# Second attention of a four-block kernel: the first batch's output projection issued inside steps 50 to 63 of the score loop instead of steps 64 to 68

## The chip, the cores and the metric

The kernel runs on one core of a Trainium2 chip, as one program of five engines (TensorE, VectorE, ScalarE, GpSimd and SyncE, in the trace PE, DVE, ACT, POOL and SP) that wait for each other through semaphores. The metric is the device time of one execution in microseconds.

## What is computed

Four blocks are applied in turn to x of 2 x 512 x 256 floats, each as `x = x + layernorm(block(layernorm(x)))`: a linear attention, a mixture of experts, a softmax attention and a second mixture of experts. The change is in the third:

```python
qkv = jnp.einsum('bsd,df->bsf', x, Wqkv) + bqkv
...
scores = jnp.einsum('bqhd,bkhd->bhqk', q, k) / np.sqrt(HEAD_DIM).astype(np.float32)
attn = jax.nn.softmax(scores, axis=-1)
out = jnp.einsum('bhqk,bkhd->bqhd', attn, v).reshape(bsz, seqlen, D_MODEL)
return jnp.einsum('bsd,de->bse', out, Wo) + bo
```

There are 32 query heads of width 8 over 8 key heads, and 512 positions in each of the 2 batches. The last line is the output projection.

## The kernel before

The 1024 rows of x are eight tiles of 128 rows; tiles 0 to 3 (TB = 4) are the first batch, 4 to 7 the second. In the softmax attention the 64 head and batch pairs are taken four at a time (GH = 4), in NG = 16 groups n, and every group has four steps c, one for each tile of queries or keys. STEPS is 64. All engines walk the same written order of steps c = 0 to 72 (END = STEPS + LAG + 3), with d = c - 6:

- `scores1(c, i)` on TensorE makes the scores of two heads (queries by keys) in one PSUM bank each, and VectorE's `maximum` (L1744) reads each for the row maxima. This ends with step 63.
- GpSimd splits the maxima, and TensorE turns them with q (`turn`, L1594: kinds "q1", "q2", "k" and "o").
- `scores2(d, i)` makes the scores again the other way round (keys by queries, maxima included), ScalarE takes exp of each (L1505), and `weigh(d - 2, half)` (L1634) multiplies by the values into one accumulating bank.
- Every fourth step ScalarE copies a finished group's sums to `oT` (L1495), TensorE turns them (kind "o"), and VectorE divides them into `xn` (`outputs`, L1751, L1752), which from here on holds the attention's output. Group 7, the first batch's last, is in `xn` at step 40.

In a step TensorE has the order scores1 of heads 0 and 1, scores2 of two heads, half a weigh, a turn where there is one, scores1 of heads 2 and 3, an "o" turn where there is one, scores2 of the other two heads, the rest of the weigh. PSUM has eight banks. Banks 0, 1, 2 and 5 (`DVE_BANKS`) form a ring in which what VectorE reads rotates: four score tiles a step and every fourth step an "o" turn. The list `FOR_DVE` is that ring's order, and `wait_bank` makes TensorE wait until the item four places earlier has been read. Banks 3, 4 and 7 are a second ring, for ScalarE.

The output projection has four pieces for each tile t: `turn_att(t)` on TensorE (L1651, two transposes of xn's tile), a copy to `xT` (`copy_att`, L1762, by VectorE for the first batch; L1508 by ScalarE for the second), `project(t)` on TensorE (L1665, two float32 products, shown by the trace as four), and `l1_y(t)` on VectorE (L1758, which adds the bias), followed by the layernorm's statistics (L666). For the first batch `turn_att(t)` stands at the end of step 64 + t and `project(t)` at the end of step 65 + t, both behind weigh, in banks 0 to 2 that the maxima no longer use. `close_stats`, GpSimd's `rstd` (L531) and `sum_x` (L695) then update x for the first batch; its statistics (`stats_x(0)`) and ScalarE's `normalise(3, 0)` (L979) come after the loop. The second batch's projection follows the loop.

Of the kernel before, what the change touches and what calls it, by code (L numbers as in the profile page):

```python
# [24 lines left out]
ALU = mybir.AluOpType  # L25
# [3 lines left out]
P = 128  # L29
B, S, D = 2, 512, 256  # L30
NT = B * S // P
TB = S // P
# [47 lines left out]
def build(nc, a, out):  # L80
    ctx = ExitStack()
    with ctx:
# [549 lines left out]
        def vector_program(dve):  # L632
# [30 lines left out]

            def tile_stats(src, t):

                mark(v.bn_stats(stat[:, t, :], src[:, t, :]))  # L666

            def close_stats(of, half):

# [5 lines left out]
                v.tensor_scalar(var[of][:, sl], mv[:, sl, 1], EPS, None, ALU.add).then_inc(var_ready[of], 1)  # L675
                v.tensor_scalar(nmean[of][:, sl], mv[:, sl, 0], -1.0, None, ALU.mult).then_inc(var_ready[of], 1)  # L676

            def y_tiles(p, tiles, make_y):

                for t in tiles:  # L680
                    make_y(t)
                for t in tiles:
                    dve.wait_ge(y_ready, p * NT + t + 1)
                    tile_stats(y, t)

            sums_from = [0, 0]

            def sum_x(p, half):

                sums_from[half] = count[0]  # L690
                dve.wait_ge(rstd_ready[1], 2 * (2 * p + half) + 1)
                if p:
                    dve.wait_ge(x_summed, (p - 1) * NT + (half + 1) * TB)
                for t in range(half * TB, (half + 1) * TB):
                    ins = v.scalar_tensor_tensor(x[:, t, :], y[:, t, :], rstd[1][:, t:t + 1], x[:, t, :],  # L695
                                                 ALU.mult, ALU.add)
                    if p == BLOCKS - 1:
                        ins.then_inc(last_summed, 1)
                    else:
                        mark(ins)  # L700

            def stats_x(half):

                for i in range(TB):
                    dve.wait_ge(dve_chain, sums_from[half] + i + 1)
                    tile_stats(x, half * TB + i)
                close_stats(0, half)

            def close_x(p, half):
# [25 lines left out]
            for half in range(2):  # L735
                for t in range(half * TB, (half + 1) * TB):
                    dve.wait_ge(x_loaded[t // 2], 16)
                    tile_stats(x, t)
# [35 lines left out]
            y_tiles(1, range(6, 8), moe_y)  # L774
            close_stats(1, 1)
            close_x(1, 1)
            l1_y = dve_l1(dve, link, mark, settle, y_tiles, close_stats, sum_x)
            stats_x(0)
            for t in range(TB, NT):
                y_tiles(2, (t,), l1_y)  # L780
            close_stats(1, 1)
# [176 lines left out]
        def scalar_program(act):  # L958
# [71 lines left out]
            turn(2, 0)  # L1030
            turn(2, 1)
            act_l1(act, normalise, turn, complete)
            normalise(3, 0)
            turn(3, 0)
            turn(3, 1)
            act_moe(act, 1, turn)
# [317 lines left out]

        STEPS = NG * TB
        LAG = 6
        PROJ_AT = STEPS
        PROJ_BANK = [ps[2]] * TB + [ps[i] for i in (2, 3, 5, 6)]
        QKV_BANK = (4, 5, 6, 7, 3, 4, 6, 6)
        QKV_AT = 3  # L1360
        DVE_BANKS, ACT_BANKS = (0, 1, 2, 5), (3, 4, 7)
# [30 lines left out]
        for c_ in range(END):  # L1392
            new = [x_ for x_ in turns_at(c_)]
            if c_ < STEPS:
                FOR_DVE += [("s1", c_ * GH + j) for j in range(GH)]
                FOR_DVE += [x_ for x_ in new if x_[0] == "o"]
            if c_ >= LAG:
                S2 = [("s2", s2_no(c_ - LAG, j)) for j in HEADS2] if c_ < STEPS + LAG else []
                FOR_ACT += S2[:2] + [x_ for x_ in new if x_[0] != "o" or x_[1] >= LATE_O] + S2[2:]
# [20 lines left out]
        def wait_bank(pe, item):  # L1420

            ring, banks = (FOR_DVE, DVE_BANKS) if item in FOR_DVE else (FOR_ACT, ACT_BANKS)
            at_ = ring.index(item) - len(banks)
            if at_ < 0:
                return
            kind, n = ring[at_]
            if kind == "s1":
                pe.wait_ge(max_read, n + 1)
            elif kind == "s2":
                pe.wait_ge(exp_ready, n + 1)  # L1430
            else:
                wait_read(pe, ring[at_])

# [33 lines left out]
        def act_l1(act, normalise, turn_copy, complete):  # L1467
            def copy_turn(what):
                kind, n = what
                act.wait_ge(turned, turn_no(what))  # L1470
                dst = kT[n] if kind == "k" else (qT1 if kind == "q1" else qT2)[n % 2]
                nc.scalar.activation(dst[:], ps[bank_no(what)], ACT.Copy).then_inc(turn_copied, 1)  # L1472

            def hi_parts(b, t):

                act.wait_ge(qkv_ready, b * TB + t + 1)
                stack_hi(nc.scalar, b, t, "k").then_inc(k_hi_made[b], 1)
                stack_hi(nc.scalar, b, t, "q").then_inc(q_hi_made[b], 1)

            act.wait_ge(l1_consts, L1_CONSTS)  # L1480
            for t in range(TB):
                hi_parts(0, t)
            for what in FIRST:
                copy_turn(what)
            normalise(2, 1)
            for c in range(END):
                d = c - LAG
                if c == 2:
                    turn_copy(2, 2)
                    turn_copy(2, 3)  # L1490
                    complete(1)
                n = (c - 12) // TB if c % TB == 0 and c >= 12 else -1
                if 0 <= n < NG:
                    act.wait_ge(av_done, (n + 1) * TB)
                    nc.scalar.activation(oT[:], ps[AV_BANK], ACT.Copy).then_inc(oT_ready, 1)  # L1495
                if d >= 3 and d < STEPS:
                    act.wait_ge(av_done, d - 2)
                for i, j in enumerate(HEADS2):
                    if i == 2:
                        for what in turns_at(c):  # L1500
                            if what[0] != "o":
                                copy_turn(what)
                    if 0 <= d < STEPS:
                        act.wait_ge(s2_made, s2_no(d, j) + 1)
                        nc.scalar.activation(pr[d % 3][:, j], s2_bank(d, j), ACT.Exp, scale=SCALE).then_inc(exp_ready, 1)  # L1505
            for t in range(TB, NT):
                act.wait_ge(attT_made, t + 1)
                nc.scalar.activation(xT[:, :, t * P:(t + 1) * P],  # L1508
                                     ps[t][:, 0:D].rearrange("p (c n) -> p c n", c=KC), ACT.Copy).then_inc(att1_copied, 1)
# [44 lines left out]
        def pe_l1(pe, turn_x):  # L1554
# [84 lines left out]
            def turn_att(t):  # L1639

                if t < TB:
                    pe.wait_ge(att_ready, LATE_O)
                    pe.wait_ge(max_read, GH * STEPS)
                    if t >= 2:
                        pe.wait_ge(att0_copied, t - 1)
                    into = ps[t % 2]
                else:
                    pe.wait_ge(att_ready, NG)
                    into = ps[t]
# [4 lines left out]
            def project(t):  # L1654

                if t < TB:
                    pe.wait_ge(att0_copied, t + 1)
                    if t:
                        pe.wait_ge(y_ready, 2 * NT + t)
                else:  # L1660
                    pe.wait_ge(att1_copied, t - TB + 1)
                    if t == TB:
                        pe.wait_ge(y_ready, 2 * NT + TB)
                for c in range(KC):
                    last = mm(PROJ_BANK[t][:, 0:D], xT[:, c, t * P:(t + 1) * P], wo1[:, c],  # L1665
                              start=(c == 0), stop=(c == KC - 1))
                last.then_inc(proj_made, 1)

# [8 lines left out]
            for c in range(END):  # L1677
# [16 lines left out]
                for what in turns_at(c):  # L1694
                    if what[0] == "o":
                        if what[1] == NG - 1:
                            keep_warm(2, SPARE)
                        turn(what)
                if c < QKV_AT:
                    keep_warm(2, 3)  # L1700
                if 0 <= d < STEPS:
# [3 lines left out]
                if 0 <= d - 2 < STEPS:  # L1705
                    if (d - 2) % TB == 0:
                        weigh(d - 2, 0)
                    weigh(d - 2, 1)
                if 0 <= c - PROJ_AT < TB:
                    turn_att(c - PROJ_AT)  # L1710
                if 1 <= c - PROJ_AT <= TB:
                    project(c - PROJ_AT - 1)
            keep_warm(4, SPARE)
            for t in range(TB, NT):
                turn_att(t)
            for t in range(TB, NT):
                project(t)

        def dve_l1(dve, link, mark, settle, y_tiles, close_stats, sum_x):
# [35 lines left out]

            def l1_y(t):
                dve.wait_ge(proj_made, t + 1)
                v.tensor_tensor(y[:, t, :], PROJ_BANK[t][:, 0:D], bo1[:], ALU.add).then_inc(y_ready, 1)  # L1758

            def copy_att(t):  # L1760
                dve.wait_ge(attT_made, t + 1)
                v.tensor_copy(xT[:, :, t * P:(t + 1) * P],  # L1762
                              ps[t % 2][:, 0:D].rearrange("p (c n) -> p c n", c=KC)).then_inc(att0_copied, 1)

            for c in range(END):
                n = (c - 12) // TB if c % TB == 0 and c >= 12 else -1
# [5 lines left out]
                if 0 <= n < NG:  # L1772
                    outputs(n)

                if 0 <= c - PROJ_AT < TB:
                    copy_att(c - PROJ_AT)
                if 1 <= c - PROJ_AT <= TB:
                    y_tiles(2, (c - PROJ_AT - 1,), l1_y)
                if c == PROJ_AT + TB:
                    close_stats(1, 0)  # L1780
                if c == PROJ_AT + TB + 1:
                    sum_x(2, 0)
            return l1_y

        @block.sync
# [42 lines left out]
```

## Time and profile before

| | us |
|---|---|
| median of 3 runs | 669.72 |
| lowest and highest | 668.78, 669.96 |
| the profiled execution, own time | 669.68 |
| its span in the trace | 667.8 |
| granted TensorE clock, mean | 0.986 of full speed |

In the trace step 50 begins at 503.3, step 64 at 541.9, and the last product of the second batch's projection ends near 571.4 us from the span's start. TensorE is busy for 92% of the span, VectorE 61%, ScalarE 49%. The profile's times are from the start of the span; the device time is 1.9 us more than the span.

### The profile page before, as it was taken

How to read it: one execution, taken by the hardware profiler on the slowest of the kernel's cores; microseconds unless marked ns; L12 is line 12 of the kernel's file. 1: busy time of each engine (PE TensorE's matmuls, PEld its weight loads, DVE VectorE, ACT ScalarE, POOL GpSimd, SP SyncE). 2: the span in 40 equal slices, each digit the busy share in tenths (PEclk: the TensorE clock that was granted, in tenths of full speed). 3: DMA queues.
4: the chain of work that ended last, by engine and by line, in shares of the span. 5: the costliest groups of instructions: out<-in, count | busy, mean ns of one | idle time of the engine just before them, and what ended most of it. 6: DMA issues, size and time to landing. Idle time of an engine off the chain costs nothing.

```text
span 667.8 us, 11795 instructions
## 1 busy us (share of the span) xinstructions
PE 617.4 (92%) x4298; PEld 408.0 (61%) x4298; DVE 404.4 (61%) x929; ACT 325.1 (49%) x645; POOL 213.2 (32%) x312
## 2 busy tenths in 40 slices
PE   3999999999999988799978999999999999989990
PEld 2887887887888785366665544444444445546660
DVE  4526705632760587533366999989998954743336
ACT  4523423433332224133215589898988875523322
POOL 5870561282073154513333031201010100331331
PEclk9999999999999999899989999999999999999996
DMA  6000200300199992222379994000000000031213
GB/s 220 33 1 33 96 1 20 107 1 1 38 283 299 78 314 77 78 58 81 105 237 346 303 180 3 1 1 2 2 1 2 1 2 1 9 104 55 81 56 126
DMA packets 69000, 57.40 MB, mean 86 GB/s; under 512 B 21520, under 2 KB 64400, under 8 KB 68944
## 3 DMA queue, kind: packets, MB, share of 16 engines
q1 hardware_dynamic: 66736, 50.60, 31.2%
q0 software_dynamic: 2208, 6.05, 2.5%
q8 instruction: 36, 0.59, 0.4%
q14 instruction: 20, 0.16, 0.1%
HBM read 30.78 MB, written 25.85 MB: 85 GB/s over the span
## 4 chain that ended last, share of the span: by engine, by line
PE 73%; DVE 16%; DMA 3%; ACT 3%; issue 2%; POOL 1%; SPq 1%; ACTq 0%; POOLq 0%; DVEq 0%
PE psum L303 9%; PE psum L305 8%; PE psum L304 8%; PE psum L1289 8%; PE psum L1634 8%; DVE mx L1744 7%; PE psum L1606 5%; PE psum L1318 5%; PE psum L1594 5%; PE psum L1619 3%; PE psum L1213 2%; DVE stat L666 2%; PE psum L1564 2%; PE psum L1282 2%; PE psum L1199 1%
## 5 line engine op out<-in xcount | busy, mean ns | idle before, releaser
L1744 DVE TENSOR_REDUCE mx<-psum 128x1 f32<-128x512 f32 x256 | 157.6, 681 | 17.6 <-PE psum L1606 17.5
L1505 ACT ACTIVATE pr<-psum 128x512 f32<-128x512 f32 x256 | 138.0, 598 | 27.9 <-PE psum L1619 26.1
L1634 PE MATMUL psum<-pr,vals 128*32 128x256 f32 x1024 | 77.6, 389 | 0.0
L1619 PE MATMUL psum<-qT,kT 32*128 32x512 f32 x256 | 76.6, 494 | 0.7 <-ACT pr L1505 0.7
L1606 PE MATMUL psum<-kT,qT 32*128 32x512 f32 x256 | 67.7, 488 | 1.7 <-ACT qT L1472 0.7
L1289 PE MATMUL psum<-w_gu,xgT 128*128 x120 | 56.4, 592 | 0.0
L624 POOL DMA_INDIRECT routed_y<-yr,xg x30 | 28.7, 958 | 86.1 <-DVE yr L876 85.5
L1606 PEld LDWEIGHTS psum<-kT,qT 32*128 32x128 f32 x256 | 26.3, 181 | 43.9 <-issue 21.4
L1546 POOL CAST mp<-mx 128x16 bf16<-128x16 f32 x16 | 3.1, 196 | 150.5 <-DVE mx L1744 150.5
L867 DVE SCALAR_TENSOR_TENSOR h<-psum,xg,sg 128x256 f32<-128x256 f32 x30 | 14.5, 484 | 49.8 <-ACT sg L1046 49.8
L1046 ACT ACTIVATE sg<-psum,xg 128x256 f32<-128x256 f32 x30 | 14.2, 474 | 60.4 <-PE psum L1289 60.4
L1013 ACT ACTIVATE q<-psum 128x512 f32<-128x512 f32 x32 | 19.1, 597 | 48.9 <-PE psum L305 48.9
L1634 PEld LDWEIGHTS psum<-pr,vals 128*32 128x32 f32 x1024 | 22.2, 108 | 29.8 <-issue 17.8
L585 POOL TENSOR_TENSOR ksum_t<-k_hi 128x1024 f32<-128x1024 f32 x8 | 19.2, 2401 | 64.6 <-DVE k_lo L814 64.4
L1619 PEld LDWEIGHTS psum<-qT,kT 32*128 32x128 f32 x256 | 34.4, 181 | 8.9 <-ACT pr L1505 4.0
L1019 ACT ACTIVATE q_hi<-q 128x512 fp32r<-128x512 f32 x32 | 20.2, 633 | 40.1 <-DVE q L845 40.1
L303 PE MATMUL psum<-kvo_hi,q_hi 128*128 128x256 f32 x128 | 38.0, 297 | 1.9 <-POOL q_lo L599 1.9
L531 POOL TENSOR_TENSOR rstd<-var,mhalf 128x4 f32<-128x4 f32 x16 | 16.5, 1028 | 64.8 <-DVE nmean L676 64.8
L304 PE MATMUL psum<-kvo_lo,q_hi 128*128 128x256 f32 x128 | 36.1, 282 | 0.0
L305 PE MATMUL psum<-kvo_hi,q_lo 128*128 128x256 f32 x128 | 36.1, 282 | 0.0
L819 DVE TENSOR_TENSOR nk<-psum,same_head 128x8 f32<-128x8 f32 x16 | 1.9, 161 | 53.0 <-PE psum L1191 53.0
L814 DVE SCALAR_TENSOR_TENSOR k_lo<-psum,k_hi 128x512 fp32r<-128x512 f32 x32 | 22.0, 689 | 18.1 <-ACT k_hi L1007 18.0
(214 smaller groups left out, 1406.6 us busy)
## 6 DMA issues: line engine op xcount, KB each, us to landing
sorted_x<-zeros SPq DMA_DIRECT2D x2, 9088.0 KB, 39.2
w_gu<-in_L_ffn_gate_w SPq DMA_DIRECT2D x16, 256.0 KB, 6.2
w_gu<-in_L_ffn_up_w SPq DMA_DIRECT2D x16, 256.0 KB, 6.3
w_d<-in_L_ffn_down_w SPq DMA_DIRECT2D x16, 256.0 KB, 6.6
xg<-sorted_x SPq DMA_DIRECT2D x30, 129.0 KB, 2.2
wk_f<-in_L_attn_Wk SPq DMA_DIRECT2D x4, 512.0 KB, 5.2
wq_f<-in_L_attn_Wq SPq DMA_DIRECT2D x4, 512.0 KB, 6.0
wv_f<-in_L_attn_Wv SPq DMA_DIRECT2D x4, 512.0 KB, 3.7
```

The source lines that it names most:

```text
L303: nc.tensor.matmul(o, lhs[0], rhs[0], start=start, stop=False, **kw)
L304: nc.tensor.matmul(o, lhs[0], rhs[1], start=False, stop=False, **kw)
L305: return nc.tensor.matmul(o, lhs[1], rhs[0], start=False, stop=stop, **kw)
L624: g.indirect_dma_start(routed_y[l][:, :], bass.IndirectOffsetOnAxis(ap=xg[r % NXG][:, D:D + 1].bitcast(U32), axis=0), yr[r % 4][:], None). ...
L1289: last = mm(ps[2 + u % 2][:], xgT[r % 2][:, c], w_gu[:, bass.ds(experts[r], 1), c, :], start=(c == 0), stop=(c == KC - 1))
L1318: last = mm(ps[6 + u % 2][:, 0:D], hT[u % 2][:, c], w, start=(c == 0), stop=(c == FC - 1))
L1505: nc.scalar.activation(pr[d % 3][:, j], s2_bank(d, j), ACT.Exp, scale=SCALE).then_inc(exp_ready, 1)
L1594: last = nc.tensor.transpose(into[:, t * P:(t + 1) * P], src, ident[:])
L1606: mm(s1_bank(c, j), qT1[n % 2][rows, t * P:(t + 1) * P], kT[n // GH][rows, :], start=True, stop=True).then_inc(s1_made, 1)
L1619: mm(s2_bank(d, j), kT[n // GH][rows, kc * P:(kc + 1) * P], qT2[n % 2][rows, :], start=True, stop=True).then_inc(s2_made, 1)
L1634: last = mm(ps[AV_BANK][j * VW:(j + 1) * VW, cols], vals[:, n // NKV * TB + kc, n % NKV // GH * GH + j, :], pr[d % 3][:, j, cols], start=( ...
L1744: v.tensor_reduce(mx[n % 2][:, t, j:j + 1], s1_bank(c, j), AX.X, ALU.max, negate=True).then_inc(max_read, 1)
```

## The change

`ATT_AT` is (50, 54, 58, 62). `turn_att(t)` and `copy_att(t)` now stand in step 50 + 4t, `project(t)`, `l1_y(t)` and its statistics in the step behind it, on TensorE between the second scores1 and the second scores2 of the step. Their results go through the maxima's ring: an "att" item behind the four score tiles of step 50 + 4t, a "proj" item behind those of the next. y of the first batch is written to `xn`, over the attention's output, instead of to `y`. `close_stats` moves to step 64, `sum_x` and `stats_x(0)` to step 65, and `normalise(3, 0)` on ScalarE stands ahead of the second batch's copies instead of behind them. The number of instructions that compute is the same.

```diff
-        PROJ_AT = STEPS
-        PROJ_BANK = [ps[2]] * TB + [ps[i] for i in (2, 3, 5, 6)]
+        ATT_AT = tuple(STEPS - 14 + 4 * t for t in range(TB))
+        PROJ_BANK = {TB + t: ps[i] for t, i in enumerate((2, 3, 5, 6))}
...
                 FOR_DVE += [x_ for x_ in new if x_[0] == "o"]
+                FOR_DVE += [("att", ATT_AT.index(c_))] if c_ in ATT_AT else []
+                FOR_DVE += [("proj", ATT_AT.index(c_ - 1))] if c_ - 1 in ATT_AT else []
...
+            elif kind == "att":
+                pe.wait_ge(att0_copied, n + 1)
+            elif kind == "proj":
+                pe.wait_ge(y_ready, 2 * NT + n + 1)
...
+            normalise(3, 0)
             for t in range(TB, NT):
                 act.wait_ge(attT_made, t + 1)
...
                 if t < TB:
-                    pe.wait_ge(att_ready, LATE_O)
-                    pe.wait_ge(max_read, GH * STEPS)
-                    if t >= 2:
-                        pe.wait_ge(att0_copied, t - 1)
-                    into = ps[t % 2]
+                    pe.wait_ge(att_ready, NKV)
+                    wait_bank(pe, ("att", t))
+                    into = ps[bank_no(("att", t))]
...
                     pe.wait_ge(att0_copied, t + 1)
-                    if t:
-                        pe.wait_ge(y_ready, 2 * NT + t)
+                    wait_bank(pe, ("proj", t))
+                    into = ps[bank_no(("proj", t))]
...
+                if c in ATT_AT:
+                    turn_att(ATT_AT.index(c))
+                if c - 1 in ATT_AT:
+                    project(ATT_AT.index(c - 1))
                 if c < QKV_AT:
                     keep_warm(2, 3)
                 if 0 <= d < STEPS:
...
-                if 0 <= c - PROJ_AT < TB:
-                    turn_att(c - PROJ_AT)
-                if 1 <= c - PROJ_AT <= TB:
-                    project(c - PROJ_AT - 1)
...
-                if 0 <= c - PROJ_AT < TB:
-                    copy_att(c - PROJ_AT)
-                if 1 <= c - PROJ_AT <= TB:
-                    y_tiles(2, (c - PROJ_AT - 1,), l1_y)
-                if c == PROJ_AT + TB:
+                if c in ATT_AT:
+                    copy_att(ATT_AT.index(c))
+                if c - 1 in ATT_AT:
+                    y_tiles(2, (ATT_AT.index(c - 1),), l1_y)
+                if c == STEPS:
                     close_stats(1, 0)
-                if c == PROJ_AT + TB + 1:
+                if c == STEPS + 1:
                     sum_x(2, 0)
+                    stats_x(0)
```

TensorE from the "q1" turn of step 50 to the end of step 51, before (names are the tiles written and read: kT,qT is scores1, qT,kT is scores2, pr,vals is weigh, ident is a turn):

```order
L1594 MATMUL psum<-ident,qs_181 128x128 x4
L1606 MATMUL psum<-kT_179,qT_1_197 128x512 x2
L1619 MATMUL psum<-qT_0_198,kT_179 128x512 x2
L1634 MATMUL psum<-pr_172,vals 32x256 x4
L1606 MATMUL psum<-kT_179,qT_1_197 128x512 x2
L1619 MATMUL psum<-qT_0_198,kT_179 128x512 x2
L1634 MATMUL psum<-pr_173,vals 32x256 x4
L1606 MATMUL psum<-kT_179,qT_1_197 128x512 x2
L1619 MATMUL psum<-qT_0_198,kT_179 128x512 x2
L1634 MATMUL psum<-pr_173,vals 32x256 x4
```

The same stretch of the changed kernel (L1658 is `turn_att`, L1671 is `project`):

```order
L1603 MATMUL psum<-ident,qs_181 128x128 x4
L1615 MATMUL psum<-kT_179,qT_1_197 128x512 x2
L1658 MATMUL psum<-ident,xn_id 128x128 x2
L1628 MATMUL psum<-qT_0_198,kT_179 128x512 x2
L1643 MATMUL psum<-pr_172,vals 32x256 x4
L1615 MATMUL psum<-kT_179,qT_1_197 128x512 x2
L1628 MATMUL psum<-qT_0_198,kT_179 128x512 x2
L1643 MATMUL psum<-pr_173,vals 32x256 x4
L1615 MATMUL psum<-kT_179,qT_1_197 128x512 x2
L1671 MATMUL psum<-wo_189,xT 128x256 x2
L1628 MATMUL psum<-qT_0_198,kT_179 128x512 x2
L1643 MATMUL psum<-pr_173,vals 32x256 x4
```

In both steps a piece of the projection has come between a scores1 and the scores2 that followed it directly.

VectorE over steps 49 to 52, before (the maxima are written as x12 and x4 since their tile changes):

```order
L1752 TENSOR_TENSOR xn_id<-psum,dn 128x4x4x8
L1744 TENSOR_REDUCE mx_190<-psum 128x1 x12
L1744 TENSOR_REDUCE mx_191<-psum 128x1 x4
L1751 RECIPROCAL dn<-psum 128x16
L1752 TENSOR_TENSOR xn_id<-psum,dn 128x4x4x8
```

And in the changed kernel:

```order
L1758 TENSOR_TENSOR xn_id<-psum,dn 128x4x4x8
L1750 TENSOR_REDUCE mx_190<-psum 128x1 x8
L1769 COPY xT<-psum 128x2x128
L1750 TENSOR_REDUCE mx_190<-psum 128x1 x4
L1765 TENSOR_TENSOR xn_id<-psum,bo_83 128x256
L666 BN_STATS stat<-xn_id 128x6
L1750 TENSOR_REDUCE mx_191<-psum 128x1 x4
L1757 RECIPROCAL dn<-psum 128x16
L1758 TENSOR_TENSOR xn_id<-psum,dn 128x4x4x8
```

The copy has come behind the eight maxima of steps 49 and 50, the bias and the statistics behind those of step 51.

TensorE in steps 65 and 66, before:

```order
L1619 MATMUL psum<-qT_0_198,kT_179 128x512 x2
L1634 MATMUL psum<-pr_171,vals 32x256 x4
L1651 MATMUL psum<-ident,xn_id 128x128 x2
L1665 MATMUL psum<-wo_189,xT 128x256 x2
L1619 MATMUL psum<-qT_1_199,kT_179 128x512 x2
L1634 MATMUL psum<-pr_172,vals 32x256 x4
```

And in the changed kernel:

```order
L1628 MATMUL psum<-qT_0_198,kT_179 128x512 x2
L1643 MATMUL psum<-pr_171,vals 32x256 x4
L1628 MATMUL psum<-qT_1_199,kT_179 128x512 x2
L1643 MATMUL psum<-pr_172,vals 32x256 x4
```

The projection's two pieces are gone from the end of step 65; steps 64 and 66 to 68 lose theirs likewise.

## Rows read from the trace of the kernel before

**Rows 1.** Windows, one each for steps 50 to 53 (TensorE, its loads, VectorE, ScalarE, GpSimd)

```profile
503.30:506.10 2.80, 2.80 (x32) 1.32 (x28) 2.46 (x5) 2.62 (x7) 0.00 (x0) 1.00 0.02 6
506.10:508.40 2.30, 2.30 (x28) 0.95 (x24) 2.30 (x5) 2.16 (x6) 0.00 (x0) 1.00 0.00 0
508.40:511.85 3.45, 3.29 (x33) 1.58 (x29) 3.42 (x8) 2.85 (x7) 1.25 (x6) 1.00 0.00 0
511.85:514.60 2.75, 2.75 (x32) 1.29 (x28) 2.12 (x5) 2.29 (x6) 0.00 (x0) 1.00 0.00 0
```

**Rows 2.** Chain that ended last, steps 50 to 52: start us, us, what

```profile
505.51 2.29 DVE mx L1744 x4
...
507.90 1.89 DVE mx L1744 x3
```

**Rows 3.** Timeline of TensorE's weight loads, step 52: start, us, idle before

```profile
509.23 0.18 PEld L1606 LDWEIGHTS psum<-kT,qT 32*128 32x128 f32 x1 [0.42 <-DVE mx L1744]
```

**Rows 4.** Waits, 502.67 to 513.98, one period: us, times, longest

```profile
DVE mx L1744 <- PE psum L1606: 1.3, 4, 0.3
```

**Rows 5.** Timeline of TensorE's products, steps 64 to 69

```profile
545.22 0.44 PE L1651 MATMUL psum<-ident,xn_id 128*128 128x128 f32 x2
545.59 0.50 PE L1619 MATMUL psum<-qT,kT 32*128 32x512 f32 x2
...
548.32 0.44 PE L1651 MATMUL psum<-ident,xn_id 128*128 128x128 f32 x2
...
549.55 0.50 PE L1619 MATMUL psum<-qT,kT 32*128 32x512 f32 x2
...
556.50 0.50 PE L1619 MATMUL psum<-qT,kT 32*128 32x512 f32 x2
556.93 0.65 PE L1594 MATMUL psum<-ident,oT 128*128 128x128 f32 x4
...
559.65 1.13 PE L1665 MATMUL psum<-wo,xT 128*128 128x256 f32 x4
560.71 0.49 PE L1619 MATMUL psum<-qT,kT 32*128 32x512 f32 x2
```

**Rows 6.** Timeline of ScalarE, steps 66 on

```profile
550.15 2.06 ACT L1505 ACTIVATE pr<-psum 128x512 f32<-128x512 f32 x4 [1.29 <-PE psum L1619]
...
564.81 0.60 ACT L1495 ACTIVATE oT<-psum 128x512 f32<-128x512 f32 x1 [1.44 <-PE psum L1634]
567.33 1.21 ACT L1508 ACTIVATE xT<-psum 128x256 f32<-128x256 f32 x4 [1.93 <-PE psum L1651]
570.26 2.08 ACT L979 ACTIVATE xn_id<-x,shift,rstd 128x256 f32<-128x256 f32 x4 [1.72 <-POOL shift L533]
```

**Rows 7.** Timeline of TensorE's products, steps 50 to 52

```profile
504.97 0.50 PE L1606 MATMUL psum<-kT,qT 32*128 32x512 f32 x2
...
505.57 0.64 PE L1634 MATMUL psum<-pr,vals 128*32 128x256 f32 x8
...
507.21 0.50 PE L1606 MATMUL psum<-kT,qT 32*128 32x512 f32 x2
...
507.87 0.64 PE L1634 MATMUL psum<-pr,vals 128*32 128x256 f32 x8
508.44 0.50 PE L1606 MATMUL psum<-kT,qT 32*128 32x512 f32 x2
...
509.83 0.66 PE L1594 MATMUL psum<-ident,oT 128*128 128x128 f32 x4
```

**Rows 8.** Timeline of VectorE, the projection's work and its end

```profile
548.79 0.42 DVE L1762 COPY xT<-psum 128x256 f32<-128x256 f32 x1 [2.68 <-PE psum L1651]
549.66 0.42 DVE L1758 TENSOR_TENSOR y<-psum,bo 128x256 f32<-128x256 f32 x1 [0.44 <-PE psum L1665]
550.12 0.43 DVE L666 BATCH_NORM_STATS2 stat<-y 128x6 f32<-128x256 f32 x1
...
568.93 0.42 DVE L1758 TENSOR_TENSOR y<-psum,bo 128x256 f32<-128x256 f32 x1
```

More of the change, by code:

```diff
@@ L664, in tile_stats @@
             def tile_stats(src, t):
-                mark(v.bn_stats(stat[:, t, :], src[:, t, :]))
+                mark(v.bn_stats(stat[:, t, :], src))
             def close_stats(of, half):
@@ L676, in close_stats, with y_of @@
                 v.tensor_scalar(nmean[of][:, sl], mv[:, sl, 0], -1.0, None, ALU.mult).then_inc(var_ready[of], 1)
+            def y_of(p, t):
+                return xn[:, t, :] if p == 2 and t < TB else y[:, t, :]
             def y_tiles(p, tiles, make_y):
@@ L683, in y_tiles @@
                     dve.wait_ge(y_ready, p * NT + t + 1)
-                    tile_stats(y, t)
+                    tile_stats(y_of(p, t), t)
             sums_from = [0, 0]
@@ L694, in sum_x @@
                 for t in range(half * TB, (half + 1) * TB):
-                    ins = v.scalar_tensor_tensor(x[:, t, :], y[:, t, :], rstd[1][:, t:t + 1], x[:, t, :],
+                    ins = v.scalar_tensor_tensor(x[:, t, :], y_of(p, t), rstd[1][:, t:t + 1], x[:, t, :],
                                                  ALU.mult, ALU.add)
@@ L705, in stats_x @@
                     dve.wait_ge(dve_chain, sums_from[half] + i + 1)
-                    tile_stats(x, half * TB + i)
+                    tile_stats(x[:, half * TB + i, :], half * TB + i)
                 close_stats(0, half)
@@ L737, in vector_program @@
                     dve.wait_ge(x_loaded[t // 2], 16)
-                    tile_stats(x, t)
+                    tile_stats(x[:, t, :], t)
                 close_stats(0, half)
@@ L776, in vector_program @@
             close_x(1, 1)
-            l1_y = dve_l1(dve, link, mark, settle, y_tiles, close_stats, sum_x)
-            stats_x(0)
+            l1_y = dve_l1(dve, link, mark, settle, y_tiles, close_stats, sum_x, stats_x, y_of)
             for t in range(TB, NT):
@@ L1032, in scalar_program @@
             act_l1(act, normalise, turn, complete)
-            normalise(3, 0)
             turn(3, 0)
@@ L1657, in project @@
                     pe.wait_ge(att0_copied, t + 1)
-                    if t:
-                        pe.wait_ge(y_ready, 2 * NT + t)
+                    wait_bank(pe, ("proj", t))
+                    into = ps[bank_no(("proj", t))]
                 else:
                     pe.wait_ge(att1_copied, t - TB + 1)
-                    if t == TB:
-                        pe.wait_ge(y_ready, 2 * NT + TB)
+                    into = PROJ_BANK[t]
                 for c in range(KC):
-                    last = mm(PROJ_BANK[t][:, 0:D], xT[:, c, t * P:(t + 1) * P], wo1[:, c],
+                    last = mm(into[:, 0:D], xT[:, c, t * P:(t + 1) * P], wo1[:, c],
                               start=(c == 0), stop=(c == KC - 1))
@@ L1717, in pe_l1, with dve_l1 @@
                 project(t)
-        def dve_l1(dve, link, mark, settle, y_tiles, close_stats, sum_x):
+        def dve_l1(dve, link, mark, settle, y_tiles, close_stats, sum_x, stats_x, y_of):
             v = nc.vector
@@ L1757, in l1_y @@
                 dve.wait_ge(proj_made, t + 1)
-                v.tensor_tensor(y[:, t, :], PROJ_BANK[t][:, 0:D], bo1[:], ALU.add).then_inc(y_ready, 1)
+                src = ps[bank_no(("proj", t))] if t < TB else PROJ_BANK[t]
+                v.tensor_tensor(y_of(2, t), src[:, 0:D], bo1[:], ALU.add).then_inc(y_ready, 1)
             def copy_att(t):
@@ L1762, in copy_att @@
                 v.tensor_copy(xT[:, :, t * P:(t + 1) * P],
-                              ps[t % 2][:, 0:D].rearrange("p (c n) -> p c n", c=KC)).then_inc(att0_copied, 1)
+                              ps[bank_no(("att", t))][:, 0:D].rearrange("p (c n) -> p c n", c=KC)).then_inc(att0_copied, 1)
             for c in range(END):
```

## The prediction, made before the result was known

> **What bounds the kernel now.** I read the windows by step first, then the chain that ended last, then the two engines' timelines around the places of the change. Four steps make a period, which repeats through the loop. Steps 50 to 53 take 2.80, 2.30, 3.45 and 2.75 us, 11.30 in all [rows 1]. The reader is to see that TensorE is busy in nearly all of it: 2.80, 2.30, 3.29 and 2.75, so 11.14 of 11.30. VectorE has 2.46 + 2.30 + 3.42 + 2.12 = 10.30. There is no engine with room for free work. The chain says which of the two leads where: it runs on TensorE in steps 49 and 50, where a step has a turn, goes over to VectorE at 505.51, stays with the maxima to 509.79, and returns to TensorE with the "o" turn at 509.83 [rows 2, 7]. VectorE waits for TensorE four times in a period, 1.3 us in total [rows 4], and none of these waits lies between 505.51 and 509.79, since that piece of the chain is VectorE's own. TensorE waits for VectorE once to any purpose, in step 52: 0.42 us ahead of the weights of the fourth score tile [rows 3].
>
> Behind step 63 there are no maxima, and TensorE leads alone: ScalarE, the only other busy engine, does its four exponentials of a step in 2.06 us and idles 1.29 before them [rows 6]. So both places, the one the work leaves and the one it comes to, are on the path. The question is only at which of them it costs more.
>
> **What the move takes away, steps 64 to 68.** From the start of a piece to the start of what follows, on TensorE: turn_att(0) alone 545.59 - 545.22 = 0.37; turn_att and project together 549.55 - 548.32 = 1.23, three times; project(3) alone 560.71 - 559.65 = 1.06 [rows 5]. Sum 0.37 + 3 x 1.23 + 1.06 = 5.12 us. What is late next is ScalarE: a step of TensorE without the pieces is what is left of the time from 549.55 to 556.50 (two steps), less two pieces: (6.95 - 2.46) / 2 = 2.24 us [rows 5], against ScalarE's 2.06, so it still fits, with 0.2 to spare instead of 1.3. In step 68 ScalarE also copies oT, 0.60 [rows 6], ahead of the "o" turn, and that no longer hides; I take 0.3 off. **Tail: -4.8 us.** Bounds: -5.1 if ScalarE never holds TensorE, -4.0 if each of steps 65 and 68, which have an extra copy of 0.60, loses most of it.
>
> **What it adds to TensorE in the loop.** Scores1 and scores2 that follow one another directly run side by side: from scores1 to the weigh behind both, 505.57 - 504.97 = 0.60 us in step 50, 507.87 - 507.21 = 0.66 in step 51 [rows 7]. A scores pair by itself, up to the next full-width transpose, takes 556.93 - 556.50 = 0.43 [rows 5]. With a piece in between, the two pairs can't share the array:
> - step 50: 0.43 + 0.37 (turn_att) + 0.43 = 1.23 instead of 0.60, +0.63;
> - step 51: 0.43 + 1.06 (project) + 0.43 = 1.92 instead of 0.66, +1.26.
>
> So +1.89 us a group for TensorE. By the Trainium skill, "TensorEngine Tiling (Array Packing)", section Key Properties, a change of tiling mode drains the array, while tiles of one mode run in parallel; by that rule each piece put between the two scores adds two such changes, where behind the weigh it only lengthened one that was there. The page gives no price; by the rows it is the 0.26 and 0.20 us of lost sharing in these two lines, and the sum does not need the rule.
>
> **What it adds to VectorE.** A copy of 0.42 behind the maxima of step 50; y of 0.42 and statistics begun 550.12 - 549.66 = 0.46 later and lasting 0.43, behind those of step 51 [rows 8]. That is 0.42 + 0.89 = 1.31 us, and it falls exactly into the stretch from 505.51 to 509.79 that is VectorE's on the path. The ring asks nothing extra: "att" waits for the first maximum of step 50, long read; "proj" for that of step 51.
>
> **The two together, group by group.** Follow step 50 from its second scores1 at 504.97, which doesn't move. Step 51 starts 0.63 late, 506.77, and its scores reach VectorE near 507.3, just behind VectorE's copy, done at 507.17 (505.51, two maxima at 0.61 each, which is 509.79 less 505.51 over seven [rows 2], and 0.42). Its four maxima end at 507.3 + 4 x 0.61 = 509.75. TensorE starts project at 506.77 + 1.0 + 0.43 = 508.2 (1.0 is half a step, scores pair and weigh, 507.21 less step 51's start at 506.1 [rows 1, 7]) and has made it 1.13 later [rows 5], at 509.4, so VectorE does y and statistics without a wait, 509.8 to 510.7. TensorE starts step 52 at 508.44 + 1.89 = 510.33 [rows 7], the first score tile is there at 510.8, and its maximum ends at 511.5. The "o" turn waits for that maximum by the ring's order: 511.5 instead of 509.83. **+1.65 us** for a group. VectorE alone, fed without a wait, would give 509.83 + 1.31, so +1.3: the lower bound. TensorE alone without any wait given back gives +1.89. The upper bound is both in series at one place: +1.89 and one more wait of VectorE of the usual 0.3 [rows 4] and what it passes on, 2.4.
>
> Groups 50, 54 and 58 cost 1.65 each. The last, 62 and 63, has no maxima behind it, so TensorE's 1.89 counts in full. **Loop: 3 x 1.65 + 1.9 = +6.85 us.** Bounds 3 x 1.3 + 1.6 = 5.5 and 3 x 2.4 + 1.9 = 9.1.
>
> **The end.** ScalarE's normalise(3, 0), 2.08 us, now stands ahead of the copies of the second batch. oT is done at 565.41, the copies began at 567.33 [rows 6]: the gap is 1.92, so the copies start 0.16 later. Its cover is that gap; were x of the first batch not ready, the copies would wait. It is: close_stats is at step 64 and the sum at 65, over 10 us earlier. stats_x(0) leaves VectorE just ahead of y(4) at 568.93, but the chain through the second batch's products holds y(4) there [rows 8]. What follows is led by the second batch's y, statistics and sum, all on VectorE in the same order, so having the first batch ready earlier gives nothing. **+0.15 us.** Taking y's place in xn costs nothing: same shapes, and its last reader, turn_att, is long done.
>
> **Sum.** -4.8 + 6.85 + 0.15 = +2.2 us. On the profiled execution's own 669.68 that is 671.9; the median of the runs shown, 669.72, is the same to 0.04.
>
> **Rivals.** 0.2% is 1.3 us, about what a measurement of this kernel can tell from no change.
> - *The ring gives more back* (same). The products share the array after all, or the shift lets VectorE's own 1.31 be the whole price. Loop 5.5, tail -5.1, end 0.15: +0.5, 670.2. For it: VectorE's and TensorE's ways to the "o" turn are only 0.3 apart. Against: the sharing is plain in the rows. Chance 0.2.
> - *More is lost in the loop, or less gained in the tail* (slower, more). Ring waits chain up: loop 8 to 9.1, or ScalarE binds the tail, -4.0. About +4.2, 673.9. For it: ScalarE has 2.62 of 2.80 in step 50 [rows 1]. Against: scores2 come later too, so its ring of banks is freer. Chance 0.2.
> - *The waits absorb the work* (faster). VectorE's 1.31 falls into its 1.3 us of waits in a period [rows 4], and TensorE pays its own pieces 1.23 less the 0.42 it waited [rows 3]: 0.81 a group. Loop 3.25, tail -4.8, end 0.15: -1.4, 668.3. It decides once a group costs under 0.8 us. Against: those waits lie in other steps than the insertions, and the ring is four deep, one step. Chance 0.08.
> - Forecast, +1.4 to +3.2: chance 0.52.
>
> The range reaches from the first rival to the second: 669.6 to 674.4. Slower by over 0.2% takes the forecast and the second rival with the edge of each: 0.70. Within 0.2%: 0.22. Faster: 0.08.
>
> **What would show it.** Right: the period with steps 50 and 51 about 1.65 us longer than 11.30, with the "o" turn coming near 511.5; scores1 to weigh near 1.2 us in step 50 and 1.9 in step 51; step 64 beginning near 548.8; then steps of 2.2 to 2.3 us, and the last product of the second batch near 573.6. Wrong: a period of 12.1 or less (absorbed), VectorE waiting over 1 us in step 51 or 52 (the rings chain up), tail steps over 2.6 us (ScalarE binds), or the mixture of experts behind it starting earlier relative to the last y.

## The result and the profile after

In runs that alternated with the kernel before, the changed kernel took 675.21 us in the median of 20 (672.43 to 679.06), and the kernel before 674.02 in the median of 20 (668.78 to 677.6). The ratio is 1.004, with a 95% interval of 1.002 to 1.0059: slower by 2.7 us, between 1.3 and 4.0. The two medians by themselves lie only 1.2 us apart and the two means 2.0, since single runs spread over 7 us in the one kernel and 9 in the other; the size of the change is therefore read from the traces below. A change of +2.2 us was forecast. The forecast of the time itself, 671.9 with 669.6 to 674.4, missed the measured 675.21, because the kernel before was not at 669.7: its three runs shown were among its fastest. This is taken up below.

The profiled execution took 673.56 us, its span is 671.8. The windows of the changed kernel for steps 50 to 53, in the columns of [rows 1] (window, length, then busy time of TensorE, its loads, VectorE, ScalarE and GpSimd, granted clock, DMA share, GB/s):

```profile
501.42:504.84 3.42, 3.42 (x34) 1.53 (x30) 3.08 (x7) 2.61 (x6) 0.00 (x0) 1.00 0.02 5
504.84:508.50 3.66, 3.66 (x32) 1.73 (x28) 3.45 (x8) 2.17 (x5) 0.41 (x2) 1.00 0.00 0
508.50:511.80 3.30, 2.93 (x32) 1.50 (x28) 2.88 (x7) 2.99 (x7) 0.84 (x4) 1.00 0.00 0
511.80:514.59 2.79, 2.79 (x32) 1.29 (x28) 2.17 (x5) 2.33 (x6) 0.00 (x0) 1.00 0.00 0
```

The four steps take 13.17 us where they took 11.30 [rows 1]: +1.87. Step 50 has 0.62 more, step 51 1.36 more, step 52 0.15 less (0.04 of that is where the window was cut: step 53 has 0.04 more). In the first two TensorE is busy all the time, so the added time is its own.

The chain that ended last shows who leads over steps 50 to 52 now, where [rows 2] had VectorE from the middle of step 50 to the middle of step 52:

```profile
503.15 0.43 PE psum L1615 x2
503.59 0.37 PE psum L1658 x2
503.95 0.42 PE psum L1628 x2
504.38 0.57 PE psum L1643 x8
504.95 0.43 PE psum L1615 x2
505.38 0.18 PE psum L1628 x2
505.56 0.57 PE psum L1643 x8
506.13 0.42 PE psum L1615 x2
506.55 1.06 PE psum L1671 x4
507.61 0.42 PE psum L1628
508.04 0.57 PE psum L1643 x8
508.61 0.48 PE psum L1615 x2
509.09 0.69 DVE mx L1750
509.78 0.04 issue
509.82 0.66 PE psum L1603 x4
```

Of seven maxima in a row one is left, the first of step 52. Each piece of the projection (L1658, L1671) stands between a scores1 (L1615) and a scores2 (L1628), which take 0.43 and 0.42 one after the other. VectorE's timeline of the same stretch, to be read beside [rows 8]:

```profile
504.82 0.41 DVE L1769 COPY xT<-psum 128x256 f32<-128x256 f32 x1
505.42 2.48 DVE L1750 TENSOR_REDUCE mx<-psum 128x1 f32<-128x512 f32 x4 [0.18 <-PE psum L1615]
507.82 0.41 DVE L1765 TENSOR_TENSOR xn_id<-psum,bo 128x256 f32<-128x256 f32 x1
508.26 0.43 DVE L666 BATCH_NORM_STATS2 stat<-xn_id 128x6 f32<-128x256 f32 x1
509.07 2.48 DVE L1750 TENSOR_REDUCE mx<-psum 128x1 f32<-128x512 f32 x4 [0.38 <-PE psum L1615]
```

VectorE makes copy, y and statistics without waiting for their inputs, and then idles 0.18 and 0.38 us until the next score tile comes. So its 1.3 us of added work is covered, by TensorE's longer steps.

The rest of the loop and what follows is compared from marks that all versions have, the starts of ScalarE's copies to oT in steps 48, 64 and 72, and VectorE's first y of the second batch:

| executions profiled | copy 48 to 64 | copy 64 to 72 | copy 72 to y(4) | sum |
|---|---|---|---|---|
| before | 44.65 | 22.67 | 4.12 | 71.44 |
| changed | 52.41 | 17.72 | 4.12 | 74.25 |
| difference | +7.76 | -4.95 | 0 | +2.81 |

The 2.81 us of the trace lie within the interval of the timed runs, 1.3 to 4.0. In the tail, the steps behind the loop, a new wait stands where the pieces were taken out. ScalarE's timeline of the changed kernel, steps 65 to 68, and TensorE's step 68:

```profile
553.25 5.43 ACT L1513 ACTIVATE pr<-psum 128x512 f32<-128x512 f32 x10
558.56 0.60 ACT L1503 ACTIVATE oT<-psum 128x512 f32<-128x512 f32 x1
```

```profile
558.25 0.50 PE L1628 MATMUL psum<-qT,kT 32*128 32x512 f32 x2
559.31 0.63 PE L1603 MATMUL psum<-ident,oT 128*128 128x128 f32 x4 [0.56 <-ACT oT L1503]
```

ScalarE runs ten exponentials without a gap, where [rows 6] had 1.29 us of idle time before four. In step 68 TensorE waits 0.56 us for its copy, and the chain runs on ScalarE from 556.60 to 559.17, in steps 67 and 68. In step 64 such a wait stands in both kernels (0.56 us before, 0.58 changed).

### The profile page after: what moved, and what is told of

It is laid out like the page before. It is cut to its first block, busy times and chain, and to the rows that moved or that the text cites. A ratio compares the mean times of both kernels' runs of the same rounds, so it can differ in the third digit from the quotient of the medians.

```text
span 671.8 us, 11795 instructions
## 1 busy us (share of the span) xinstructions
PE 621.3 (92%) x4298; PEld 410.1 (61%) x4298; DVE 399.2 (59%) x929; ACT 325.3 (48%) x645; POOL 213.3 (32%) x312
## 4 chain that ended last, share of the span: by engine, by line
PE 74%; DVE 12%; DMA 4%; ACT 3%; issue 2%; POOL 2%; another core or an unknown queue 1%; SPq 0%; ACTq 0%; POOLq 0%; DVEq 0%
PE psum L303 9%; PE psum L305 8%; PE psum L304 8%; PE psum L1643 8%; PE psum L1291 8%; DVE mx L1750 6%; PE psum L1615 6%; PE psum L1320 5%; PE psum L1603 5%; PE psum L1628 3%; PE psum L1215 2%; DVE stat L666 2%; PE psum L1573 2%; PE psum L1201 1%; PE psum L1208 1%
## 5 line engine op out<-in xcount | busy, mean ns | idle before, releaser
L1628 PE MATMUL psum<-qT,kT 32*128 32x512 f32 x256 | 75.8, 494 | 0.5 <-ACT pr L1513 0.5
L1615 PE MATMUL psum<-kT,qT 32*128 32x512 f32 x256 | 66.8, 487 | 1.4 <-ACT qT L1480 0.7
L1615 PEld LDWEIGHTS psum<-kT,qT 32*128 32x128 f32 x256 | 26.1, 181 | 42.6 <-issue 22.6
L1628 PEld LDWEIGHTS psum<-qT,kT 32*128 32x128 f32 x256 | 34.1, 181 | 10.8 <-issue 5.6
L1291 PEld LDWEIGHTS psum<-w_gu,xgT 128*128 128x128 f32 x120 | 23.5, 196 | 16.6 <-issue 14.8
```

The costliest lines, as they stand in the source:

```text
L1291: last = mm(ps[2 + u % 2][:], xgT[r % 2][:, c], w_gu[:, bass.ds(experts[r], 1), c, :], start=(c == 0), stop=(c == KC - 1))
L1615: mm(s1_bank(c, j), qT1[n % 2][rows, t * P:(t + 1) * P], kT[n // GH][rows, :], start=True, stop=True).then_inc(s1_made, 1)
L1628: mm(s2_bank(d, j), kT[n // GH][rows, kc * P:(kc + 1) * P], qT2[n % 2][rows, :], start=True, stop=True).then_inc(s2_made, 1)
```

## Experiments

The pieces were moved, thinned out and put back one at a time. Sums are from copy 48 to y(4) in the profiled execution, as in the table above. Ratios are of runs against the kernel before on the same chip, with their 95% intervals; they resolve little under 0.3%. The sums of two executions of one version agree to 0.05 us where the clock did not fall between the marks.

**The kernel before, again** (before_again). No edit.

> The kernel before, unchanged, against itself. It tells how far two profiles of one program lie apart and in which stages. Expected: ratio 1.000 within 0.2%; in the trace, from step 50 to step 64 38.5 us and from step 64 to the last oT copy 22.95 us, both to 0.1, while the mixtures of experts and the stages before step 50 may differ by 1 to 3 us. Rival theory, that the 3 us by which the changed kernel is longer behind the second batch's y belong to the change: then these stages agree here to 0.3 us as well.

Measured: ratio 1.0004 (0.9977 to 1.003), 44.68 + 22.67 + 4.13 = 71.48 us. From y(4) to the end of the span this execution took 101.6 us and the first one 98.9, the same program. So the 3.1 us by which the changed kernel's profile is longer there say nothing of the change; the kernel `behind`, which has the move too, took 99.1 there in its second profile. The windows of the first execution, then of this one, over the same 15 us of the second mixture of experts:

```profile
600.00:615.00 15.00, 15.00 (x61) 9.55 (x60) 5.10 (x13) 5.12 (x15) 1.91 (x2) 1.00 0.19 54
```

```profile
597.60:612.60 15.00, 15.00 (x56) 9.65 (x56) 4.58 (x11) 4.48 (x13) 1.06 (x2) 0.93 0.17 45
```

The granted clock there is 1.00 of the upper level, 2.4 GHz, in the one and 0.93 in the other, which has 56 products in the 15 us instead of 61.

**The end put back** (undo_end, and undo_end_again for a second profile). One part of the change undone:

```diff
+            stats_x(0)
             for t in range(TB, NT):
...
             act_l1(act, normalise, turn, complete)
+            normalise(3, 0)
...
-            normalise(3, 0)
             for t in range(TB, NT):
                 act.wait_ge(attT_made, t + 1)
...
                     sum_x(2, 0)
-                    stats_x(0)
```

> The changed kernel with stats_x(0) back behind the loop and normalise(3, 0) back behind the second batch's copies. My theory (the end gives and costs nothing): steps 50 to 64 take 46.0 us as changed, 4.1 us from the last oT copy to the first y of the second batch, total the changed kernel's within 0.2%, so +0.4% against before. Rival (the earlier normalise delays or helps the second batch): a difference of 0.5 us or more between oT and the last y, or in the time from there to the second half's router transposes.

Measured: 52.39 + 18.90 + 4.12 = 75.41 us, ratio 1.0028 (1.0001 to 1.0055). Loop and end as expected, but the tail 1.18 longer, which neither theory had. Its window around the oT turn of step 68:

```profile
558.40:562.40 4.00, 3.95 (x27) 1.70 (x28) 0.55 (x2) 1.97 (x4) 0.00 (x0) 0.57 0.02 4
```

The clock was at its lower level, 1.2 GHz, for most of these 4 us, and 16 products of weigh took 1.94 us where they take 1.07. It fell at 558.6, just behind the wait of 0.55 us in step 68. Whether that belonged to this version, a second profile of the same kernel tells.

> The same kernel as undo_end, whose tail took 18.90 us instead of 17.72 in an execution in which the granted clock fell to half for 3.4 us at 569 us of the record, around the oT turn of step 68. Theory: that fall is chance of the execution and not of this kernel, so a tail without it takes 17.7 us. Rival: stats_x(0) and normalise in their old places cost 1.2 us, and the tail is 18.9 again at full clock.

```profile
559.90:563.90 4.00, 3.44 (x34) 1.61 (x33) 0.55 (x2) 3.13 (x7) 0.00 (x0) 1.00 0.01 4
```

Measured: 52.41 + 17.73 + 4.13 = 74.27, the changed kernel's sum to 0.02. So the end's part of the change is worth nothing either way, and the fall was not there in every execution of this version.

**Statistics made later** (stats_late).

```diff
                 if c - 1 in ATT_AT:
-                    y_tiles(2, (ATT_AT.index(c - 1),), l1_y)
+                    l1_y(ATT_AT.index(c - 1))
                 if c == STEPS:
+                    y_tiles(2, range(TB), lambda t: None)
                     close_stats(1, 0)
```

> The changed kernel with the four bn_stats of the first batch's y taken out of steps 51 to 63 and made together in step 64; VectorE has 0.43 us less in each group. Theory A (TensorE's pieces and the lost sharing are the price, VectorE idles 0.38 us before step 52's maxima): steps 50 to 64 stay at 46.0 us, the idle time grows to 0.8. Theory B (VectorE's 1.31 us a group is the price): 4 x 0.4 less, 44.4 us, and a total 1.6 us shorter.

Measured: 52.39 + 17.74 + 4.13 = 74.26, ratio 1.0033 (1.0007 to 1.0059). VectorE's idle time ahead of step 52's maxima grew from 0.38 to 0.84 us, as expected, and four times 0.43 us less work for it inside the loop changed nothing. Theory B falls: in the changed kernel TensorE's way is the price.

**Behind weigh** (behind, and behind_again for a second profile). The edit, on TensorE alone:

```diff
-                if c in ATT_AT:
-                    turn_att(ATT_AT.index(c))
-                if c - 1 in ATT_AT:
-                    project(ATT_AT.index(c - 1))
                 if c < QKV_AT:
                     keep_warm(2, 3)
...
                     weigh(d - 2, 1)
+                if c in ATT_AT:
+                    turn_att(ATT_AT.index(c))
+                if c - 1 in ATT_AT:
+                    project(ATT_AT.index(c - 1))
```

> The changed kernel with turn_att and project at the end of their steps, behind weigh, instead of between scores1 and scores2. Theory A (each piece between the two scores also costs their running side by side, 0.26 and 0.20 us): TensorE pays 0.37 + 1.06 = 1.43 us a group instead of 1.89, so steps 50 to 64 take 44.2 us against 46.0 as changed and 38.5 before, and the total is about 1 us over before. Theory B (only VectorE's work counts): 46.0 unchanged. Scores1 and scores2 in steps 50 and 51 again 0.60 to 0.66 us together.

Measured: 50.03 + 19.92 + 4.13 = 74.08, ratio 1.0021 (0.9995 to 1.0047), again with a fall of the clock in the tail, at 0.55 from 559.6 to 563.4. The second profile had none:

> The same kernel as behind, whose tail took 19.92 us with the clock at half for 3.4 us. Theory: at full clock the tail takes 18.6 us as in the run with late statistics, so the whole from step 48's oT copy to the second batch's first y is 72.8, 1.3 us over before.

Measured: 50.01 + 18.58 + 4.12 = 72.71, so 1.54 us under the changed kernel and 1.27 over before, as expected. From the start of step 50 to that of step 64 the two executions took 44.96 and 44.95 us, where theory A had 44.2 and theory B 46.0: of the 1.84 us that A expected to save by there 1.09 came. The last product stands behind copy 64 here, so the loop's part looks shorter and the tail's longer than in the changed kernel by about that product. The scores are side by side again, and a new wait has come. Chain of the first execution, steps 51 and 52:

```profile
506.11 0.42 PE psum L1615
506.54 0.31 PE psum L1628 x2
506.84 0.57 PE psum L1643 x8
507.41 1.07 PE psum L1671 x4
508.49 0.02 issue
508.51 0.44 DVE xn_id L1765
508.95 0.02 issue
508.97 0.04 DVE stat L666
509.00 0.31 issue
509.31 0.69 DVE mx L1750
```

The product is done at 508.49, the y waits for it, the statistics follow, and the maximum that the "oT" turn waits for begins only at 509.31. Step 53 starts 1.67 us later than in the kernel before, against 1.87 as changed: of TensorE's own saving of 0.46 us, 0.20 is left in each of the first three groups. In the last group, with no maxima behind its product, the saving is whole, 0.49 by the same marks. The remaining 0.43 is gained in step 64: the product lies beside ScalarE's work there, and of the 0.58 us for which TensorE waited for ScalarE in the changed kernel 0.16 are left.

**Behind weigh, with late statistics** (behind_stats). Both edits above.

> The pieces behind weigh, and the first batch's four statistics made in step 64. Behind alone cost 1.67 us a group at the turn of step 52 although TensorE paid only 1.43, because y waited 0.45 us for the product at the step's end and the statistics then held up step 52's first maximum by 0.36. Theory: both engines lead in turn, and with this cover gone the statistics do count: 1.67 - 0.36 = 1.3 us a group at the turn, 50.1 - 3 x 0.36 = 48.9 us between the oT copies of steps 48 and 64. Rival (VectorE never counts, as in the run with late statistics alone, which changed nothing): 50.0 as behind.

Measured: 48.92 + 18.59 + 4.13 = 71.64, ratio 1.0007 (0.9982 to 1.0033). The edit that was worth nothing above is worth 1.07 us here. VectorE does count once TensorE's way is shorter: the chain has gone back to the product, the next scores and one maximum.

**Product and next transposes in one step** (joined). On top of behind:

```diff
+        PROJ_STEP = ATT_AT[1:] + (STEPS - 1,)
...
-                if c - 1 in ATT_AT:
-                    project(ATT_AT.index(c - 1))
+                if c in PROJ_STEP:
+                    project(PROJ_STEP.index(c))
```

The ring's list and VectorE's y follow to the same steps.

> The pieces behind weigh, and project(t) in the same step as turn_att(t + 1), as the kernel before has them in steps 65 to 67; the last product at the end of step 63. Theory A (TensorE's time is the price, and it is the same wherever the pieces stand): 0.37 + 3 x 1.23 + 1.06 = 5.1 us in the loop, about what the tail gives back, total within 0.2% of before. Theory B (the loop is led by both engines in turn, and here VectorE waits for the transposes, copies, waits for the product and makes y and statistics before the next maximum): about 1.6 us a group, 6.4 in all, total 0.2 to 0.3% over before.

Measured: 49.30 + 18.58 + 4.12 = 72.00, ratio 1.0001 (0.9973 to 1.0029). Theory B's step is seen, VectorE waits for the product and then goes through y and statistics, in step 54:

```profile
519.12 0.41 DVE L1770 COPY xT<-psum 128x256 f32<-128x256 f32 x1
519.88 0.42 DVE L1766 TENSOR_TENSOR xn_id<-psum,bo 128x256 f32<-128x256 f32 x1 [0.35 <-PE psum L1672]
520.34 0.43 DVE L666 BATCH_NORM_STATS2 stat<-xn_id 128x6 f32<-128x256 f32 x1
520.69 4.85 DVE L1751 TENSOR_REDUCE mx<-psum 128x1 f32<-128x512 f32 x8
```

The sum is 0.56 over before. From step 50 to step 64 it took 44.23 us, 5.7 over before, between A's 5.1 and B's 6.4, and the totals of both lie within what the runs can tell.

**The same with late statistics** (joined_stats).

> Both mends together: turn_att(t + 1) and project(t) in one step behind weigh, and the four statistics in step 64. In the joined run VectorE led behind each pair of pieces (copy, 0.35 of waiting, y, statistics, maximum), so with the statistics gone the loop should lose 0.3 to 0.4 us in each of the last three groups: 49.30 - 1.1 = 48.2 us between the oT copies of steps 48 and 64, 18.6 for the tail, and 0.5 us less than the kernel before from step 48 to the second batch's first y. Rival (TensorE's 5.1 us are the floor): 48.9 or more, and no gain. The total is within 0.2% of before either way.

Measured: 48.65 + 18.61 + 4.12 = 71.38, ratio 0.9998 (0.9966 to 1.003). The loop lost 0.65 of the 1.1 us forecast. The marks say where: of the periods from oT copy to oT copy, 12.86 became 12.51 and 12.35 became 12.03, but 12.50 stayed. So the size for one group was right and the number of groups, three, was wrong; these marks show two. The rival was nearly right: steps 50 to 64 took 43.57 us, 5.05 over before, which is theory A's 5.1. The sum is 0.06 under before, which no run can tell from it. No version of the move that was tried beats the kernel before by more than the traces resolve.

**One step earlier** (one_earlier).

```diff
-        ATT_AT = tuple(STEPS - 14 + 4 * t for t in range(TB))
+        ATT_AT = tuple(STEPS - 15 + 4 * t for t in range(TB))
```

> As changed, but one step earlier: turn_att in steps 49, 53, 57 and 61, project in 50, 54, 58 and 62, where TensorE has turns of q and leads the chain, and VectorE has its waits. Theory (the pieces break the side by side of the two scores wherever they stand): TensorE pays 0.63 + 1.26 = 1.9 us, 1.9 us a group as changed or slightly more, 52.4 us between the two oT copies. Rival (the price comes from the steps in which VectorE leads): clearly less, 51.2 or under.

Measured: 52.84 + 17.72 + 4.13 = 74.69, in one execution. The work falls where VectorE has its waits, and costs 0.44 more than as changed and than was expected. The rival, that VectorE's waits could take it in, is gone.

**A wait filled in the kernel before** (hole). turn_att(0) from the end of step 64 to ahead of its oT turn:

```diff
                             keep_warm(2, SPARE)
+                        if c == PROJ_AT:
+                            turn_att(0)
                         turn(what)
...
-                if 0 <= c - PROJ_AT < TB:
+                if 0 < c - PROJ_AT < TB:
                     turn_att(c - PROJ_AT)
```

> The kernel before with turn_att(0) moved from the end of step 64 to just ahead of its oT turn, where TensorE waits 0.56 us for ScalarE's copy. Theory: the 0.37 us of the piece lie beside that wait, so 22.67 us between the oT copies of steps 64 and 72 become 22.3 to 22.4. Rival (the wait is not there to be filled, since ScalarE would be later too): 22.67 unchanged.

```profile
541.38 0.41 PE L1651 MATMUL psum<-ident,xn_id 128*128 128x128 f32 x2 [0.45 <-DVE mx L1746]
541.62 0.60 PE L1594 MATMUL psum<-ident,oT 128*128 128x128 f32 x4
```

TensorE waits 0.45 us ahead of the transposes now, for the last maximum, and goes from them to the oT turn without a wait. Measured: 44.66 + 22.30 + 4.12 = 71.08, in one execution: 0.36 under before, the whole piece. It is the shortest sum of the study, and the only one in which a piece went to where TensorE waits. Of the total it is 0.05%, which the timed runs could not show.

**The changed kernel, again** (after_again). No edit.

> The changed kernel, unchanged. Expected 52.4 and 17.7 us between the oT copies of steps 48, 64 and 72, unless TensorE's clock falls in the tail as in the runs undo_end and behind, which would add about 1.2 us. Total 0.3 to 0.4% over before.

Measured: 52.40 + 17.72 + 4.13 = 74.25, the first profile's sum. Ratio 1.0027 (0.9994 to 1.006).

## Why the prediction was right and wrong

**The base failed, and with it the time.** The step that failed is the last of the sum, "on the profiled execution's own 669.68 that is 671.9": it took three runs for the kernel's time. In the 20 runs that alternated with the changed kernel the base was 674.02, and the same sum on it gives 676.2, within 1 us of the 675.21 measured. The kernel before has since had a median of 674.02 (20 runs), 671.87 (35), 671.09 (23) and 671.85 (23), with single runs from about 668 to 678 (one of 970 aside). The slower runs go with a lower granted clock: in the last of these sets the five with a mean of 0.986, that of the first profile, took 668.9 to 669.9 us, and the five at 0.973 or under 675.2 to 677.9. The first profile had no fall of the clock in the second mixture of experts. In the 14 profiles the time from y(4) to the end was 98.9 to 99.1 us in three, 100.1 to 100.5 in three and 101.6 to 102.1 in eight, whichever the version. Ten of the 14 had a fall of the clock in that part, the eight longest among them; the three shortest had none. The range covered the uncertainty of the difference only. The difference that was timed, 0.4%, is +2.7 us against a forecast of +2.2, and the traces' is +2.8.

**Right, but for one wait: both places are on the path.** TensorE's added time in the loop counted, and so did what it shed in the tail; the sign of the forecast stands. That "TensorE leads alone" behind step 63 leaves out its wait of 0.56 us for ScalarE's copy in step 64, the room that `hole` filled.

**Right: the lost side by side.** "Step 50 +0.63, step 51 +1.26": scores1 to weigh is 504.31 - 503.08 = 1.23 us in step 50 and 507.97 - 506.06 = 1.91 in step 51 of the changed kernel's TensorE timeline, 0.60 and 0.66 before [rows 7]:

```profile
503.08 0.50 PE L1615 MATMUL psum<-kT,qT 32*128 32x512 f32 x2
...
504.31 0.64 PE L1643 MATMUL psum<-pr,vals 128*32 128x256 f32 x8
504.88 0.50 PE L1615 MATMUL psum<-kT,qT 32*128 32x512 f32 x2
...
505.49 0.64 PE L1643 MATMUL psum<-pr,vals 128*32 128x256 f32 x8
506.06 0.49 PE L1615 MATMUL psum<-kT,qT 32*128 32x512 f32 x2
...
507.97 0.64 PE L1643 MATMUL psum<-pr,vals 128*32 128x256 f32 x8
```

Its price is isolated only in part: behind weigh it is regained, at 1.54 us in all instead of the 1.84 of four groups at 0.46, since another wait takes its place. The Trainium skill ("TensorEngine Tiling (Array Packing)", Key Properties) says that a change of tiling mode drains the engine. Whether such a drain or the plain succession of the two pairs costs the 0.26 and 0.20 us, no run separates. By the rows' shapes a piece behind weigh adds one change as well (128*32, 128*128, 32*128 instead of 128*32, 32*128), where the prediction had it only lengthen one.

**Off in size: a group.** +1.65 was forecast, +1.87 came. Half of the difference is the other pair of step 51, which the sum left as it was: from its first scores1 to its weigh 505.49 - 504.88 = 0.61, where before it was 0.50. A likely cause, not tested, is that scores2 there finds its bank later, since ScalarE takes step 50's last scores 2.95 us behind the step's start (504.41 - 501.46) instead of 2.23 (505.57 - 503.34). The other half lies between step 52's start and its "o" turn, 509.82 - 508.54 = 1.28 us where the forecast had 511.5 - 510.33 = 1.17. With the last group, the loop cost 7.5 us to the start of step 64 (46.04 against 38.52) instead of 6.85. A group in behind_stats cost 1.3 as well (12.61 against 11.30), but that is not the lower bound "from VectorE alone" come true: VectorE had 0.43 us less to do there than the bound took.

**Right: the tail.** -4.8 forecast, -4.7 from step 64's start, -4.95 from copy 64. ScalarE took over in steps 67 and 68, and TensorE waits for its copy; that took 0.4 off the 5.12 us of the pieces, where the forecast took 0.3. The steps are 1.06 to 1.18 us a half, 2.2 each, as forecast.

**Wrong but small: the end.** +0.15 forecast for normalise ahead of the copies, 0 measured (4.12 and 4.12). The second batch's copies start 2.52 us behind the start of the oT copy in both (567.33 - 564.81 and 568.25 - 565.73): normalise began at 566.22, a tenth before the oT copy had ended by the rows, where the sum had it begin at its end, and just filled the gap. undo_end_again shows the same 4.13.

**The rivals.** "The waits absorb the work" is refuted by the loop and by one_earlier; its sum also took 1.23 us for TensorE's two pieces, which stand apart and take 0.37 + 1.06 = 1.43. "The ring gives more back", with VectorE's 1.31 as the whole price, is refuted for the change by stats_late, which left the time where it was. "More is lost in the loop" had the right sign of what was missed.

## What to carry to other kernels

Moving work from one stretch to another gained nothing here, where the same engine was on the path in both; what paid was a wait: the one piece set into TensorE's wait for oT cost nothing there. So look for a wait of the engine that is on the path before moving its work. Where two engines lead in turn, a cover that hides a term in one arrangement is gone in the next: the same four statistics were worth 0 us in one arrangement, 1.07 in another and 0.62 in a third. A piece put between two products that run side by side cost its own time and what they shared. And before a time is forecast rather than a difference, more than three runs of the base are needed.

## What was not expected of the hardware

In every one of the 14 profiles TensorE's granted clock falls from 2.4 to 1.2 GHz two to four times ahead of the program's last 15 us, for 3.4 or 6.8 us: in all of them near 280 us from the span's start and once between 337 and 349, and beyond that in places that differ between executions of one program. One such fall in the second mixture of experts went with 2.7 us more behind y(4) (before against before_again). That is more than the fall itself explains: 3.4 us at half the clock can cost TensorE 1.7 us at most, an estimate from its length. And undo_end took 100.3 us behind y(4) without any fall in that part, so something else moves this time too, which no run here isolates. In the attention's tail falls were seen in two of the eleven profiles in which TensorE waits for ScalarE's copy in step 68, at 1.2 us in undo_end against its second profile, and in none of the three in which it doesn't. That is too few to say that the wait brings them about; two further executions (behind_stats and joined) had a fall near 383 us from the span's start, ahead of anything that was changed.
